# Row maxima from two 64-row groups of TensorE, and VectorE as the evictor of two kinds of loop product

## What is computed

```python
def _L0_attn_ref(x, Wq, Wk, Wv, Wo, bo):
    ...
    q = (x @ Wq).reshape(b, s, N_HEADS, HEAD_DIM)
    k = (x @ Wk).reshape(b, s, N_HEADS, HEAD_DIM)
    v = (x @ Wv).reshape(b, s, N_HEADS, HEAD_DIM)
    dot = jnp.einsum('bihd,bkhd->bhik', q, k)
    w = jax.nn.softmax(dot / jnp.sqrt(jnp.float32(HEAD_DIM)), axis=-1)
    a = jnp.einsum('bhij,bjhd->bihd', w, v)
    a = a.reshape(b, s, N_HEADS * HEAD_DIM)
    return a @ Wo + bo
```

## Time and profile before

| | us |
|---|---|
| median of 3 runs | 913.68 |
| lowest, highest | 911.87, 914.02 |
| profiled execution, its own time | 913.78 |
| its span, first to last instruction | 912.0 |
| PE busy | 747.2 (82%), 9062 matmuls |
| ACT busy | 682.5 (75%), 841 instructions |
| POOL busy | 648.2 (71%), 368 instructions |
| DVE busy | 531.0 (58%), 863 instructions |
| mean granted TensorE clock | 0.920 of full speed |

### The profile page before, as it was taken

One profiled execution on the slowest core, in us unless ns is written; L12 is line 12 of the kernel. 1 busy time (PEld: TensorE's weight loads), 2 busy tenths in 40 slices (PEclk: granted clock), 3 DMA queues, 4 the chain that ended last, 5 costly groups with the idle time before them and its releaser, 6 DMA issues. The chain is left out here.

```text
span 912.0 us, 21703 instructions
## 1 busy us (share of the span) xinstructions
PE 747.2 (82%) x9062; PEld 511.6 (56%) x9062; DVE 531.0 (58%) x863; ACT 682.5 (75%) x841; POOL 648.2 (71%) x368
## 2 busy tenths in 40 slices
PE   1889999999999999999999999999973006999500
PEld 0346566666656666666666666666663005899400
DVE  4946666666666666666666676666257402555222
ACT  2889999899999989999999999999975002444202
POOL 2899889788878978888898888989961771000173
PEclk9989999999999999999999999999995556999855
DMA  4603072220303122130311303020032011222112
GB/s 164 142 2 71 4 167 45 52 53 23 71 5 74 25 50 48 29 71 4 74 34 42 71 4 74 20 56 2 5 120 71 27 53 47 57 58 59 37 53 75
DMA packets 44288, 48.79 MB, mean 54 GB/s; under 512 B 6816, under 2 KB 28832, under 8 KB 44064
## 3 DMA queue, kind: packets, MB, share of 16 engines
q1 hardware_dynamic: 41472, 42.84, 19.1%
q0 software_dynamic: 2048, 4.23, 1.5%
q10 hardware_dynamic: 672, 0.33, 0.2%
HBM read 13.81 MB, written 8.33 MB: 24 GB/s over the span
## 5 line engine op out<-in xcount | busy, mean ns | idle before, releaser
L474 POOL TENSOR_TENSOR pl<-p,ph 128x1024 f16<-128x1024 f32 x256 | 541.0, 2133 | 76.5 <-ACT ph L379 76.3
L521 DVE TENSOR_REDUCE mx<-mps 128x1 f32<-128x1024 f32 x249 | 304.3, 1222 | 134.5 <-PE mps L238 131.9
L378 ACT ACTIVATE p<-sps,escale 128x1024 f32<-128x1024 f32 x256 | 286.9, 1121 | 37.4 <-PE sps L218 28.5
L379 ACT ACTIVATE ph<-sps,escale 128x1024 f16<-128x1024 f32 x256 | 285.2, 1114 | 0.0
L306 PE MATMUL pair_bank<-v,ph 128*128 128x65 f16 x2048 | 214.7, 193 | 0.0
L308 PE MATMUL pair_bank<-v,ph 128*128 128x64 f16 x2048 | 214.5, 195 | 0.0
L310 PE MATMUL pair_bank<-v,pl 128*128 128x65 f16 x2048 | 214.1, 192 | 0.0
L306 PEld LDWEIGHTS pair_bank<-v,ph 128*128 128x128 f16 x2048 | 190.9, 96 | 31.0 <-POOL pl L474 0.9
L308 PEld LDWEIGHTS pair_bank<-v,ph 128*128 128x128 f16 x2048 | 190.1, 97 | 30.3
L217 PE MATMUL sps<-q_hh,k_hl 128*128 128x512 f16 x512 | 195.1, 381 | 5.9 <-ACT ph L379 5.3
L218 PE MATMUL sps<-q_lm,k_h 65*128 65x512 f16 x512 | 195.7, 382 | 0.0
(11 more groups left out here) (182 smaller groups left out, 925.8 us busy)
## 6 DMA issues: line engine op xcount, KB each, us to landing
q_hh<-hi SPq DMA_DIRECT2D x60, 128.0 KB, 2.3
q_lm<-lo SPq DMA_DIRECT2D x30, 128.0 KB, 2.3
k_h<-hi SPq DMA_DIRECT2D x30, 128.0 KB, 2.4
k_hl<-hi SPq DMA_DIRECT2D x29, 128.0 KB, 2.4
k_hl<-lo SPq DMA_DIRECT2D x29, 128.0 KB, 2.5
w<-in_w1T SPq DMA_DIRECT2D x8, 352.0 KB, 4.5
sorted<-pad SPq DMA_DIRECT2D x1, 2535.0 KB, 14.8
xb<-sorted SPq DMA_DIRECT2D x39, 65.0 KB, 1.9
```

What stands on the lines that cost most here:

```text
L378: nc.scalar.activation(p32[:, n % 4, :], sps[:, n % 2, :], ACT.Exp, bias=EXP_BIAS, scale=escale[:, 0:1])
L379: nc.scalar.activation(ph[:, n % 4, :], sps[:, n % 2, :], ACT.Exp, bias=EXP_BIAS, scale=escale[:, 0:1]).then_inc(s_exp, 1)
L474: nc.gpsimd.tensor_tensor(pl[:, n % 4, :], p32[:, n % 4, :], ph[:, n % 4, :], ALU.subtract).then_inc(s_subp, 1)
L521: nc.vector.tensor_reduce(mx[:, i // TB, i % TB:i % TB + 1], src, AX.X, ALU.max).then_inc(s_mx, 1)
```

## The change

It does three things. The maxima of a tile of queries become two matmuls of 64 rows each: the first uses rows 0 to 63 (query high, key high, keys 0 to 511), the second rows 64 to 127 (the query's second copy, and a new tile `k_far` with the high part of keys 512 to 1023). The low part of the key no longer enters the maxima. In the built program each of the two uses an array tile of 64 by 128, at row 0 and at row 64. Of the other matmuls in either program the transposes of the maxima (L274 before) use tiles of 128 by 32, and all the rest use 128 by 128. `spread_head` gets a seventh DMA, of half size, for `k_far`. And VectorE evicts both halves of the loop's pieces (`take_piece`) and the turned outputs.

```diff
-    return 96 * pairs - (64 if a == 0 else 0)
+    return 16 * 7 * pairs - (64 if a == 0 else 0)
...
+        k_far = sb("k_far", [P, 2, 2, S // 2], F16)
...
-                                 (k_hl[HD:P, par, a, :], lo[r, 1, :]), (k_h1[0:HD, par, a, :], hi[r, 1, :])):
+                                 (k_hl[HD:P, par, a, :], lo[r, 1, :]), (k_h1[0:HD, par, a, :], hi[r, 1, :]),
+                                 (k_far[HD:P, par, a, :], hi[r, 1, S // 2:])):
                     sp.dma_start(dst, src).then_inc(s_head[a], 16)
...
-                for kh in range(2):
-                    mm = nc.tensor.matmul(out[:, kh * 512:(kh + 1) * 512], q_hh[:, par, a, qt * P:(qt + 1) * P],
-                                          k_hl[:, par, a, kh * 512:(kh + 1) * 512], start=True, stop=True)
+                queries = slice(qt * P, (qt + 1) * P)
+                nc.tensor.matmul(out[:, 0:512], q_hh[0:HD, par, a, queries], k_hl[0:HD, par, a, 0:512],
+                                 start=True, stop=True)
+                mm = nc.tensor.matmul(out[:, 512:1024], q_hh[HD:P, par, a, queries], k_far[HD:P, par, a, :],
+                                      start=True, stop=True)
                 mm.then_inc(s_maxmm, 1)
...
-                    if kind == "project":
-                        round_piece(k, job + number, pp + 2)
-                    if kind == "turn":
-                        take_turned(job + number)
...
+            def take_turned(job):
+                dve.wait_ge(s_misc, job + 1)
+                nc.vector.tensor_scalar(aoT[:].rearrange("p q t -> p (q t)"), misc[:], vinv[:, 0:1], None,
+                                        ALU.mult).then_inc(s_used, 1)
+
+            def take_piece(k, job, pp):
+                if k == 0:
+                    for a in range(2):
+                        dve.wait_ge(s_head[a], spreads(a, pp + 2))
+                dve.wait_ge(s_misc, job + 1)
+                nc.vector.tensor_scalar(hi[:, k // 2, k % 2 * 512:(k % 2 + 1) * 512], misc[:], QK_UNIT, None,
+                                        ALU.mult).then_inc(s_hi, 1)
+                rest_of_piece(k, 4 * pp + 9 + k)
...
+                    if kind == "turn":
+                        take_turned(job + number)
...
                     if kind == "project":
-                        rest_of_piece(k, 4 * pp + 9 + k)
+                        take_piece(k, job + number, pp)
```

More of the change, by code:

```diff
@@ L172, in _ @@
             sp.dma_start(q_lm[0:HD, 0, 0, :], lo[0:HD, 0, :]).then_inc(s_head[0], 16)
+            sp.dma_start(k_hl[HD:P, 0, 0, :], lo[0:HD, 1, :]).then_inc(s_head[0], 16)
             sp.dma_start(k_h1[0:HD, 0, 0, :], hi[0:HD, 1, :]).then_inc(s_head[0], 16)
@@ L395, in round_piece @@
                                      scale=QK_UNIT).then_inc(s_hi, 1)
[L397 to L401, removed]
             def value_rows(j):
@@ L432, in _ @@
             act.dma_start(k_hl[0:HD, 0, 0, :], hi[0:HD, 1, :]).then_inc(s_first, 16)
-            act.dma_start(k_hl[HD:P, 0, 0, :], lo[0:HD, 1, :]).then_inc(s_first, 16)
+            act.dma_start(k_far[HD:P, 0, 0, :], hi[0:HD, 1, S // 2:]).then_inc(s_first, 16)
             for k in range(4):
```

## The result

| | before | after |
|---|---|---|
| median, us | 913.29 | 922.99 |
| lowest and highest, us | 911.87 to 914.02 | 922.89 to 924.02 |
| span of the profiled execution, us | 912.0 | 920.5 |

Both medians are of four runs. The ratio is 1.0111, with a 95% interval of 1.0093 to 1.0128: the changed kernel is **1.1% slower**, 9.7 us. The forecast said 893.5, so its sign is wrong. All ratios are of undisturbed executions; one of the twelve of the halves alone took 1904.13 us, for a reason that isn't known, and is left out of its ratio.

What follows compares the result with a forecast made beforehand. The prediction took PE to bound the loop. Savings of 18.2 us over pairs 0 to 13 and 1.9 in pair 14 took the span from 912.0 to 891.9; with the execution's 1.8 over its span, forecast 893.5, range 880 to 930.

Steps and rivals of the forecast that it cites:

- PE bounds the loop: In the loop, PE's own work fills the whole pair of heads, 38.95 us by sum against 38.98 in the trace.
- The halves start together: In each slot's maxima, the second matmul starts 0.03 us behind the first, saving 0.18 a slot, 2.9 a pair.
- A change of tiling costs nothing: Going into halves and back at each slot's maxima was priced at 0, with 0.165 us a change as upper end.
- The prediction's rival, 0.165 a change: Each change of the rows' tiling at every slot's maxima drains PE, 0.165 us a change: 955 us, chance 0.14.
- DVE's prices: On DVE, evicting 512 columns from PSUM was taken as 0.69 us; the gained evictions add 4.2 a pair.
- DVE delays slots 4 and 8: DVE's added high half delays normalising, so PE waits 0.6 us for `O` at each of slots 4 and 8.
- the wait at slot 11: Behind slot 9's piece DVE finishes slot 10's maxima late, so PE waits 0.3 us a pair for `mps`.
- Turned outputs, the seventh DMA, ACT's relief: Turned outputs on DVE and a head's seventh DMA cost nothing; relieving ACT of 3.8 us a pair can't help alone.
- ahead of and behind the loop: Early maxima ahead of the loop, where PE idles half the time, and everything behind it change the time by 0.
- The sum: A full pair gains 1.3 us, pairs 0 to 13 18.2, pair 14 1.9 and pair 15 0: 20.1 together.
- the rival in which the halves don't run at once: In the loop PE keeps 38.95 us a pair and waits 0.43 at slots 4 and 8: 926 us, chance 0.13.
- The small bubble: Each tiling change at the maxima costs 0.03 to 0.06 us, shrinking the gain: 903 to 917 us, chance 0.15.

Runs made afterwards that it cites:

- the halves alone: The changed kernel with both kinds of eviction back on ACT, keeping the 64-row maxima, `k_far` and its DMA: 910.98 us, ratio 0.9968 to the kernel before.
- the evictions alone and the high half first: The changed kernel with full-depth maxima as before and the high half evicted on DVE ahead of the slot's reduction of maxima: 918.42 us, ratio 1.0057.
- The one-half run: The changed kernel with evictions back on ACT and both maxima matmuls on rows 0 to 63, so they can't overlap: 965.57 us, ratio 1.0573.
- the columns run: The kernel before with each maxima matmul split into two of 64 query columns at full depth (tiles 128 by 64): 969.6 us, ratio 1.0617.
- the evictions alone: The changed kernel with full-depth maxima as before, no `k_far` and no seventh DMA, so only evictions move to DVE: 931.35 us, ratio 1.0199.

## Why the prediction was wrong

**PE bounds the loop: right.** Before, 38.95 by the sum; the changed pair is 38.98 + 0.81. The run with the evictions alone and the high half first relieves ACT by 3.8 a pair, and no slot of it is shorter.

**The halves start together: right, and a bit better than taken.** Steps of 0.00 to 0.01, where 0.03 was taken from the earlier trace rows; the saving is 0.215 a slot, not 0.18. The one-half run gives 0.213 from the whole time. The Trainium skill's 4 ns between starts (TensorE: Matmul & The Clock Gate, Part 3, Packing small matmuls) agrees with the trace as far as its hundredths go.

**A change of tiling costs nothing: this is the step that failed.** The prediction took 0 from the row of L274 and kept 0.165 as the upper end. The runs show 0.10 a change, 0.21 a slot, which cancels the saving of 0.215 almost to the last hundredth. The prediction noted that L274 changes columns and not rows; but that difference isn't the one that matters, as the columns run shows. L274 misled since a float32 transpose doesn't pay at all, and the trace of before has no other operation with a tiling of its own in the loop. The prediction's rival, 0.165 a change, was too high a price for the right mechanism, and its break-even of 0.055 a change lies well under the measured 0.10. The Trainium skill's rule "Changing tiling mode (not just tile) drains the TensorE" (TensorEngine Tiling (Array Packing), Key Properties) agrees with the runs, in that a change costs time: 0.10 us for rows, for columns and for small tiles. Whether the array drains in it, no run shows. The prediction's "for the column tiling the trace disagrees with it" was a wrong reading of an operation that doesn't pay.

**DVE's prices: right.** The high half takes 0.681, taken as 0.69. The turned output takes 0.746; 0.69 was taken for the shape (and 0.65 stands in DVE's sum), some 0.06 to 0.1 too little, and nothing waits for it.

**DVE delays slots 4 and 8: the right mechanism, 0.6 in place of 0.43.** Step by step: reduction at 0.43 (0.45 in the prediction), high half 1.58 (1.60), low half 2.29 (2.32), reciprocal 2.90 (2.91), multiply 3.11 (3.12). DVE's chain was right to 0.03. Two terms of the wait were off, and they pull apart. PE comes later than predicted, since its slots are 2.04 long and not 1.86: it wants `O` at 3.25 and not at 2.97. And from the multiply's end to the value matmul it takes 0.15, for which the prediction had 0.04 (3.54 to 3.58), so PE goes on at 3.68. The wait is 0.43 and not 0.6; with a hand-over of 0.04 it would have been 0.3 by estimate. That hand-over is also why the 0.43 expected of the evictions alone came out as 0.52. Because the slots are longer, **the wait at slot 11 doesn't come**: from the start of slot 9, by the prediction's own count, PE wants `mps` back at 2.04 + 2.14 = 4.18 and no longer at 3.82, and DVE's 4.15 is in time. With the evictions alone DVE is 0.21 later, and there the wait comes, with 0.17.

**Turned outputs, the seventh DMA, ACT's relief: right; ahead of and behind the loop, nearly.** With 2 high halves and both turned outputs left on DVE the kernel runs at 912.09. That run has all seven DMAs of a head too. Slots 11 to 15 keep their lengths in after. The 0.27 ahead of the loop and the 1 us behind it were taken as 0.

**The sum.** Per pair the prediction had -2.9 + 1.6 = -1.3. It is -3.4 (0.215 x 16) + 3.4 (2 changes x 16 x 0.105) + 0.8 = +0.8. The saving and the price of the changes were each judged alone; the price, known only from a row of another kind of operation, decided the sign. Pair 14 saves 0.18 and not 1.9. Nearest in number was the rival in which the halves don't run at once (926, with waits of 0.43), but its mechanism isn't what happened, so the nearness is luck. What happened is the rival with a price for each change, at some two thirds of its price, and with waits that come to 0.86 a pair, for its 0.6. The small bubble (up to 0.06) and the drain (0.165) had the measured 0.10 between them, and no case stood there.

**What stays open**: what exactly fills the 0.10 of a change of tiling (the load that isn't hidden, 0.10 long in its row, fits in size, and nothing here tells it from the array running empty); the 0.10 that slot 0 of some pairs gains from the halves; what the 1 us is that comes back behind the loop; why a float32 transpose pays nothing, and whether a larger one would. None of the versions is much better than before: the halves alone are 0.3% faster.

## What to carry to other kernels

Running two half-depth matmuls at once pays only if enough tiled work stands between the change into the tiling and the one out of it: here the two changes cost as much as one 512-column matmul, so one pair of halves between them breaks even. A second pair costs 0.22 where two full-depth matmuls take 0.43, so by estimate it would gain 0.21. When a row is to price a new operation, ask in which respects it is of the same kind; here a transpose told nothing of a matmul. When work moves to an engine with time to spare, look at which instruction stands behind it in that engine's order: the same 0.68 us costs 10 us of the kernel ahead of a result that PE waits for, and next to nothing where the engine was idle. And when a hand-over between engines is on the path, count the waits of the instruction that goes on: with a second wait it came 0.15 us behind the release, and with one 0.06.

## What the runs showed of the hardware

- A change of the array's tiling costs about 0.10 us at the clock of 2.4 GHz, into halves and out of them, for rows (64 by 128), columns (128 by 64) and an 8-column stationary; it doesn't depend on whether 65 or 512 columns were in flight (0.12 for 0.03, 0.31 for 0.215), nor on whether two or four tiled matmuls stand between the changes. The weight load behind a change isn't hidden: it starts with its matmul.
- Two matmuls in different row halves and banks start 0.00 to 0.01 apart (383.77 and 383.78 in after) and each takes 0.39, about its usual 0.38.
- A float32 transpose with 8 columns pays none of this: 0.03 ahead and 0.10 behind, in before. The plain float32 matmul in its place starts 0.12 behind the value matmul, and the next follows 0.31 later, its two passes included.
- PE's first instruction behind a wait for DVE starts 0.05 to 0.06 us behind the end of DVE's where it has one wait (433.99 to 434.04 in the evictions alone, high half first), and 0.15 behind it where it has a second one and the first stands as an instruction of 51 ns (387.30 to 387.45 in after, 433.48 to 433.63 in the evictions alone).
- The two edits don't add in time: -2.7 and +17.6 alone, +9.7 together.
